# A two-layer attention and expert kernel: low halves by TensorE, zeros and bias moved, first steps reordered

## The reference, cut to what matters

```
x = x + L0_xattn(layernorm(x), ctx)   # cosine similarity of 64-wide projections: dots / (|v| |t|)
x = x + L0_ffn(layernorm(x))          # sigmoid gate, 8 experts in 4 groups, 2 groups then top 2 kept, shared expert
x = x + L1_xattn(layernorm(x), ctx)   # softmax cross attention, 16 heads of 8, biases on q, k, v, o
x = x + L1_ffn(x)                     # causal attention along the batch axis, then 8 GELU experts of 256, top 2
```

## Time and profile before

| | us |
|---|---|
| median of three runs | 919.15 (914.24 to 921.09) |
| the profiled execution's own time | 918.29 |
| its span, first to last instruction | 916.4 |
| busy: PE / DVE / ACT / POOL | 738.4 / 659.9 / 394.2 / 219.5 |
| mean granted TensorE clock, share of full | 0.928 |

### The profile page before, as it was taken

How to read it: one execution, slowest core, us unless ns; L and a number is a source line. 1 busy time by engine, 2 the same in 40 slices (tenths; PEclk the granted TensorE clock), 3 DMA queues, 4 the chain that set the end, 5 groups by cost and what they waited for, 6 DMA issues and landing times. The chain is left out here.

```text
span 916.4 us, 26258 instructions
## 1 busy us (share of the span) xinstructions
PE 738.4 (81%) x10100; PEld 550.8 (60%) x10100; DVE 659.9 (72%) x1808; ACT 394.2 (43%) x749; POOL 219.5 (24%) x338
## 2 busy tenths in 40 slices
PE   2568897887768787778888657787775999999997
PEld 1335555554456665666666425555553888888886
DVE  4479898887846888888888467887645656666653
ACT  2122222222313555555555435665542555545553
POOL 4333333335422023213100164334002001111100
PEclk9969999998787999999999859999996999999999
DMA  3000000320141211221120000000000000000000
GB/s 97 12 19 20 13 20 20 82 43 5 40 125 44 74 43 45 69 74 44 50 65 13 13 1 4 4 5 4 4 6 1 1 13 11 11 11 11 11 12 13
DMA packets 33082, 26.41 MB, mean 29 GB/s; under 512 B 9741, under 2 KB 29913, under 8 KB 32985
## 3 DMA queue, kind: packets, MB, share of 16 engines
q1 hardware_dynamic: 29944, 24.07, 9.9%
q10 hardware_dynamic: 3040, 0.98, 0.4%
HBM read 13.51 MB, written 7.34 MB: 23 GB/s over the span
## 5 line engine op out<-in xcount | busy, mean ns | idle before, releaser
L1826 PEld LDWEIGHTS bank<-w2r,hme 128*128 128x128 f32 x1024 | 132.3, 192 | 15.8 <-ACT hme L1679 1.4
L1826 PE MATMUL bank<-w2r,hme 128*128 128x128 f32 x1024 | 135.5, 276 | 0.0
L1679 ACT ACTIVATE hme<-bank,b 128x512 f32<-128x512 f32 x128 | 86.4, 687 | 96.3 <-PE bank L97 96.2
L960 ACT ACTIVATE P<-bank 128x512 f32<-128x512 f32 x128 | 76.7, 599 | 95.4 <-PE bank L1097 95.4
L1776 DVE SCALAR_TENSOR_TENSOR Xq<-bank,wgte,Xq 128x128 f32 (+1 forms) x256 | 72.0, 343 | 51.9 <-PE bank L1826 38.4
L1022 DVE TENSOR_SCALAR bank<-bank 128x512 f32<-128x512 f32 x128 | 89.0, 695 | 26.7 <-PE bank L1088 26.7
L1030 DVE TENSOR_REDUCE mx<-bank 128x4 f32<-128x512 f32 x128 | 87.1, 681 | 6.0 <-PE bank L1070 6.0
L1097 PE MATMUL bank<-mT,negsel 128*128 128x128 f16 x512 | 50.6, 222 | 44.6 <-DVE bank L1022 41.8
L502 ACT ACTIVATE w2r<-bank 128x512 f32<-128x512 f32 x40 | 23.9, 597 | 126.3 <-PE bank L803 92.2
L1097 PEld LDWEIGHTS bank<-mT,negsel 128*128 128x128 f16 x512 | 31.8, 98 | 55.7 <-issue 40.7
L814 PE MATMUL bank<-w_raw,hm 128*128 128x128 f32 x320 | 51.4, 313 | 8.6 <-DVE X L728 8.6
(11 more groups left out here) (375 smaller groups left out, 1796.3 us busy)
## 6 DMA issues: line engine op xcount, KB each, us to landing
cross_q<-qh SPq DMA_DIRECT2D x24, 128.0 KB
Q<-cross_q SPq DMA_DIRECT2D x8, 384.0 KB, 3.6
X<-in_x SPq DMA_DIRECT2D x8, 256.0 KB, 2.8
Xq<-X SPq DMA_DIRECT2D x32, 64.0 KB
cross_k<-kh SPq DMA_DIRECT2D x16, 128.0 KB
Yq<-Y SPq DMA_DIRECT2D x32, 64.0 KB
out_x<-Xq SPq DMA_DIRECT2D x32, 64.0 KB, 1.7
cload<-in_ctx SPq DMA_DIRECT2D x8, 192.0 KB, 2.6
```

The costliest lines, as they stand in the source:

```text
L960: act.activation(P[j][:], TB[j % 2][:], ACT.Exp, scale=SCALE).then_inc(s["p_ready"], 1)
L1679: act.activation(hm[:, p % HR], UP[p % RING][:], ACT.Gelu_apprx_tanh, bias=b1[:, p:p + 1]).then_inc(s["gelu"], 1)
L1826: last = pe.matmul(Y[e % 2][:, cols], hm[:, p % HR, cols], w2r[:, p], start=(p % 2 == 0 and i == 0), stop=(p % 2 == 1), skip_group_check=True)
```

## The change

Seven edits:

1. Layer 0, start: DVE's low halves of the expert and gate weights go from ahead of the first statistics to step -2, part 0 (`fill(0)`).
2. Layer 0: the zeros of K[0] and Q, six fills, go from POOL's `ahead` to DVE in step -2, part 1 (`fill(1)`).
3. Layer 0, step -1 alone: PE, ACT and DVE do `route(0, p)` ahead of `prep(1, p)`, and PE does `prep(1, 3)` (the broadcast of the norms) behind the routing's part 4.
4. The four copies of the last group to Xq go from the end of layer 0's SP list to the head of the cross attention's, ahead of the load of w2 and the gather.
5. Cross attention, chunks 2 to 7: the low halves of K and Q are made without DVE. PE leaves the bank's accumulation open, adds a product of the negated identity (`less`, a new fp16 tile that POOL writes) with the high half, ahead of the fourth score quarter, and ACT copies the bank to fp16 at the end of its step, behind the third exponential. New semaphores k_less and q_less.
6. The expert bias goes from step -1 to step 32, one before the last, into bank S0, with a wait for the last maxima; ACT's copies go to step 33.
7. POOL writes `less` between the V tiles and `ones16`.

```diff
@@ -148 +148 @@
     }
-    c["s"] = room.sems("""small_const w_hi w_lo zeros ones_v stats_a stats_b stats_c stats_d xn_ready xT_psum
+    c["s"] = room.sems("""small_const w_hi w_lo zeros ones_v k_less q_less stats_a stats_b stats_c stats_d xn_ready xT_psum
         xT_hi xT_lo k_psum k_hi k_lo k_out k_in q_psum q_hi q_lo q_out q_in v_psum v_ready s_psum s_max m_ready mT_psum mT_ready
@@ -183 +183 @@
-def cross_project(pe, c, cT, ident, ps, n, i):
+def cross_project(pe, c, cT, ident, ps, n, i, whole=True):
@@ -195 +195 @@
         pe.wait_ge(s["xT_lo"], n + 1)
-        split_product(pe, ps[:], [w[:] for w in c["wk"]], [tok(t, n) for t in cT]).then_inc(s["k_psum"], 1)
+        split_product(pe, ps[:], [w[:] for w in c["wk"]], [tok(t, n) for t in cT], stop=whole,
+                      skip_group_check=not whole).then_inc(s["k_psum"], 1)
     elif i == 2:
         pe.wait_ge(s["k_lo"], n + 1)
-        split_product(pe, ps[:], [w[:] for w in c["wq"]], [x[:] for x in c["xh"]]).then_inc(s["q_psum"], 1)
+        split_product(pe, ps[:], [w[:] for w in c["wq"]], [x[:] for x in c["xh"]], stop=whole,
+                      skip_group_check=not whole).then_inc(s["q_psum"], 1)
@@ -363 +365 @@
                 sp.dma_start(tile, source).then_inc(s["layer1_loaded"], 16)
-            for g in range(G):
+            for g in range(G - 1):
                 sp.wait_ge(s["x2_ready"], g + 1)
@@ -440 +442 @@
                 cross_normalise(pool, c, X, 0)
-                for t in c["K"][0] + c["Q"]:
-                    last = pool.memset(t[:].bitcast(mybir.dt.uint32), 0)
-                last.then_inc(cs["zeros"], 1)
                 cross_normalise(pool, c, X, 1)
@@ -500 +499 @@
                         act.activation(sg[:, p % 2, :], GP[p % 2][:], ACT.Silu).then_inc(s["sg_ready"], 1)
+                    if isinstance(g, int) and g == -1:
+                        route(g + 1, p)
                     if has(g + 2):
                         prep(g + 2, p)
-                    if has(g + 1):
+                    if has(g + 1) and not (isinstance(g, int) and g == -1):
                         route(g + 1, p)
@@ -543 +544 @@
             dve.tensor_tensor(wt0[1][:], P0[0:CT, DV:2 * DV], wt0[0][:], ALU.subtract).then_inc(s["w0t_split"], 1)
-            dve.wait_ge(s["w0_split"], 1)
-            dve.tensor_tensor(w0[1][:], w_raw[:, 0:2], w0[0][:], ALU.subtract)
-            dve.tensor_tensor(gw[1][:], gw_raw[:], gw[0][:], ALU.subtract).then_inc(s["w0_split"], 1)
...
             dve.wait_ge(s["consts"], 6)
@@ -558 +555 @@
                 last.then_inc(s["mv" + k], 1)
...
+            def fill(p):
...
+                if p == 0:
+                    dve.wait_ge(s["w0_split"], 1)
+                    dve.tensor_tensor(w0[1][:], w_raw[:, 0:2], w0[0][:], ALU.subtract)
+                    dve.tensor_tensor(gw[1][:], gw_raw[:], gw[0][:], ALU.subtract).then_inc(s["w0_split"], 1)
+                elif p == 1:
+                    for t in c["K"][0] + c["Q"]:
+                        last = dve.memset(t[:].bitcast(mybir.dt.uint32), 0)
+                    last.then_inc(cs["zeros"], 1)
@@ -663 +671 @@
                             dve.tensor_tensor(hm[:, p, :], sg[:, i, :], UP[:], ALU.mult).then_inc(s["hm_ready"], 1)
+                    if isinstance(g, int) and g == -2:
+                        fill(p)
+                    if isinstance(g, int) and g == -1:
+                        route(g + 1, p)
                     if has(g + 2):
@@ -823 +835 @@
                         up(g, p)
+                    if isinstance(g, int) and g == -1:
+                        route(g + 1, p)
+                        if p != 3:
+                            prep(g + 2, p)
+                        if p == 4:
+                            prep(g + 2, 3)
+                        continue
                     if has(g + 2):
@@ -875 +894 @@
         ones16 = sb("ones16", [128, 128], F16)
+        less = sb("less", [128, 128], F16)
+        kh, qh = c["kh"], c["qh"]
         c["K"][1] = [sb(f"K1_{j}", [128, 16 * S], F16) for j in range(U)]
@@ -912 +933 @@
+            for b in range(B - GB, B):
+                sp.dma_start(keep["Xq"][b::32], X[:, b, :]).then_inc(keep["xq_in"], 16)
             w2 = keep["w"]["w2"]
@@ -932 +955 @@
             last.then_inc(s["ones_v"], 1)
+            pool.tensor_scalar(less[:], ident[:], -1.0, None, ALU.mult)
             pool.memset(ones16[:], 1.0).then_inc(s["small_const"], 1)
@@ -986 +1010 @@
                     exp(b, 2)
+                low(n + 2, i)
...
+            def low(n, i):
...
+                if i == 1 and chunk(n):
+                    act.wait_ge(s["k_less"], n - 1)
+                    act.activation(kh[1][:], PB[:], ACT.Copy).then_inc(s["k_lo"], 1)
+                elif i == 2 and chunk(n):
+                    act.wait_ge(s["q_less"], n - 1)
+                    act.activation(qh[1][:], PB[:], ACT.Identity, bias=bq_raw[:]).then_inc(s["q_lo"], 1)
...
                 act.wait_ge(s["bias_psum"], 1)
-                act.activation(ex["b1"][:], F[:, 0:2 * NE], ACT.Copy)
-                act.activation(ex["rb"][:], F[:, 2 * NE:3 * NE], ACT.Copy).then_inc(s["bias_ready"], 1)
+                act.activation(ex["b1"][:], S0[:, 0:2 * NE], ACT.Copy)
+                act.activation(ex["rb"][:], S0[:, 2 * NE:3 * NE], ACT.Copy).then_inc(s["bias_ready"], 1)
...
             def prepare(n, i):
-                if n == 0 and i == 0:
+                if 4 * n + i == B + 1:
                     expert_bias()
@@ -1011 +1045 @@
             def prepare(n, i):
-                if i < 3 and chunk(n + 2):
+                if i == 0 and chunk(n + 2):
                     cross_low(dve, c, bq_raw, PB, n + 2, i)
@@ -1070 +1104 @@
                 last.then_inc(s["s_psum"], 1)
-                if b == 0:
-                    bias(j)
...
-            def bias(j):
...
-                for p in range(4 * j, 4 * j + 4):
-                    last = pe.matmul(F[:, p:p + 1], w1r[:, p], lnb2[:], start=True, stop=True)
-                if j == U - 1:
-                    last = pe.matmul(F[:, 2 * NE:3 * NE], lnbr[:], rT[:], start=True, stop=True)
-                    last.then_inc(s["bias_psum"], 1)
...
+            def bias():
...
+                for p in range(2 * NE):
+                    pe.matmul(S0[:, p:p + 1], w1r[:, p], lnb2[:], start=True, stop=True)
+                pe.matmul(S0[:, 2 * NE:3 * NE], lnbr[:], rT[:], start=True, stop=True).then_inc(s["bias_psum"], 1)
@@ -1111 +1141 @@
                 if i < 3 and chunk(n + 2):
-                    cross_project(pe, c, cT, ident, PB, n + 2, i)
+                    cross_project(pe, c, cT, ident, PB, n + 2, i, False)
                 elif i == 3 and chunk(n + 1):
...
                     last.then_inc(s["v_psum"], 1)
...
+            def subtract(n, i):
...
+                if i == 1 and chunk(n):
+                    pe.wait_ge(s["small_const"], 2)
+                    pe.wait_ge(s["k_hi"], n + 1)
+                    pe.matmul(PB[:], less[:], kh[0][:], start=False, stop=True, skip_group_check=True
+                              ).then_inc(s["k_less"], 1)
+                elif i == 2 and chunk(n):
+                    pe.wait_ge(s["q_hi"], n + 1)
+                    pe.matmul(PB[:], less[:], qh[0][:], start=False, stop=True, skip_group_check=True
+                              ).then_inc(s["q_less"], 1)
@@ -1141 +1183 @@
                     score_t(b, 1)
+                if b == B:
+                    pe.wait_ge(s["s_max"], U * B)
+                    bias()
                 if has(b - 2):
@@ -1158 +1203 @@
+                subtract(b // 4 + 2, b % 4)
                 if has(b1):
@@ -1167 +1213 @@
                     if b == 1:
-                        pe.wait_ge(s["bias_ready"], 1)
                         pe.wait_ge(s["small_const"], 2)
```

## The result

The changed kernel is faster by 2.9%. It takes 890.66 us (median of 4 runs, 889.09 to 892.03), beside 917.25 for the kernel before in the same measurement: ratio 0.9707, 95% interval 0.9661 to 0.9754. A second measurement on another occasion gives 891.67 and 0.9722 (0.9677 to 0.9767). Three executions far above all others of their kernel (996.84 us of the changed kernel in that second measurement, 948.08 of e_zeros, 1396.67 of the kernel before) are left out of every median and ratio of this document. The prediction was 898 with 889 to 907. The forecast gain was 21 us, the measured one 25 to 27.

What follows compares the result with a forecast made beforehand. The prediction took DVE to set the cross attention's step and a chain across PE, ACT, DVE and POOL to bound layer 0. Its terms summed to -21.0 us, from 918.3 to 897.3, given as 898 with range 889 to 907.

Steps and rivals of the forecast that it cites:

- Bound: Cross attention's steady stretch: DVE, in use 41.8 of 50 us, sets the step, and ACT has room.
- Start, -2.0: Layer 0's start: statistics ahead of the weight splits run at about 8.8 instead of 10.87, gaining 2.0 us.
- Step -1, +2.1: Layer 0, step -1: routing ahead of similarity makes the context ready 2.1 us later, a loss of 2.1 us.
- Rival (c): Layer 0: routing ahead costs step -1 nothing and step 0 starts 1 us sooner; whole 895 us, chance 0.13.
- The zeros, 0 and -4.0: Layer 0: fills cost nothing on DVE at the start; without POOL's fills step G-2 gains 4.0 us.
- rival (e): Layer 0's start: the moved fills make DVE hold the squares of group 0, +2.6; whole 901 us, chance 0.04.
- End of layer 0, -4.4: Boundary to the cross attention: SP's four copies move behind it, gaining 4.4 us.
- Start of the cross attention, -5.5: Without 34 bias passes between the first score quarters, the maxima's transpose comes sooner, gaining 5.5 us.
- Twelve steps, -10.9: Cross attention, steps 1 and 2 over six chunks: K's and Q's low halves off DVE gain 10.9 us.
- (a): Cross attention: steps don't shorten, because PE waiting for ACT replaces DVE; whole 909 us, chance 0.11.
- (d): Cross attention: PE's new wait for ACT drops its clock to 1.2 GHz; whole up to 942 us, chance 0.04.
- Bias at the end, +3.7: Cross attention's end: 34 bias passes take 4.05 us at full clock, net loss 3.7; at half clock 7.3.

Runs made afterwards that it cites:

- e_zeros: Changed kernel with the six zero fills back on POOL in step G-2 of layer 0: 896.25 us, ratio 0.9787.
- e_lows: Changed kernel with the low halves of K and Q in the cross attention back on DVE: 903.97 us, ratio 0.9860.
- e_low0: e_best with the third low half (transposed x, step 0 of each chunk) off DVE, result not the reference's: 869.82 us, ratio 0.9488.
- e_split: Changed kernel with DVE's subtractions for the low weight parts back ahead of the first statistics: 894.66 us, ratio 0.9755.
- e_prep: Changed kernel with step -1 of layer 0 back in its old order, similarity ahead of routing: 893.23 us, ratio 0.9753.
- e_copies: Changed kernel with the last group's four copies of X back ahead of the boundary to the cross attention: 897.59 us, ratio 0.9779.
- e_bstart: Changed kernel with the 34 bias passes back at the start of the cross attention: 893.96 us, ratio 0.9729.
- e_best: Changed kernel with step -1 in its old order and the bias spread over the cross attention's last eight steps: 886.45 us, ratio 0.9662.
- e_bias: Changed kernel with the 34 bias passes spread over the last eight steps of the cross attention: 890.00 us, ratio 0.9718.

## Why the prediction was right, step by step

- **Bound.** DVE sets the step of the cross attention, ACT and PE have room: shown by e_lows (12 us) and by e_low0.
- **Start, -2.0.** First statistics 1.7 to 2.1 us sooner, first addition 1.2 to 2.4 (e_split; and e_prep's 96.6 beside 98.19 and 99.01 of the kernel before). Right in mechanism, about right in size; the share of the clock in e_split's 1.2 is open.
- **Step -1, +2.1.** Right, and by the step that the forecast gave: the context is turned 2.2 us later, the first addition comes 2.7 later (e_prep). The two first terms nearly cancel, as the sum had it: 99.01 and 98.19 before, 99.15 and 99.53 after. Rival (c) is refuted at that place. Its mark in my own list was a clamp near 51.6; found were 51.17 and 51.61.
- **The zeros, 0 and -4.0.** Fills on DVE hidden (e_zeros, first addition unchanged); rival (e) didn't occur. The step with the stall is 4.05 shorter between the first profiles, 3.0 between the second, and 3.4 by e_zeros: right in mechanism, but the size is not fixed, since the stall is as long as what is left of the train (2.79 in the second profile of the kernel before). That is longer than the one instruction of the rule with which the forecast explained it; the last section comes back to this.
- **End of layer 0, -4.4.** 4.7 to 4.9, shown by e_copies.
- **Start of the cross attention, -5.5.** 6.3 to the transpose, 6.45 to the second clamp: the size was 0.8 to 0.95 too small, inside its bounds.
- **Twelve steps, -10.9.** 11.2 between the first profiles, 14.3 between the second ones. At the same amount of half clock it is 11.0 to 11.3, so the term was right; what the second pair has on top is the clock's. From the second chunk on steps 1 and 2 are at 6.52 to 6.58 and 6.53 to 6.54, except step 1 where the clock falls in step 0 (8.07 and 8.13 in the first profile, 8.12 in the second). The forecast read only a step 1 of 7.41; in the other places of that profile where the clock fell it took 7.90 to 8.47. Rivals (a) and (d) are refuted: the steps that the edit reaches are at 6.5, the clock is 0.98 and 0.99 there.
- **Bias at the end, +3.7.** The mis-sized term: 4.1 to 6.4. The passes themselves were sized rightly, 3.9 us wherever they ran at full clock. What failed is the step "here PE is at full clock" for the time behind it: the clock fell to 1.2 GHz while the passes ran or about 1 us behind them, and what follows ran at that level, which it did not in the kernel before (2 to 3 of its 13.4 to 13.7 us at half clock, 11.0 and 6.4 of the 19.8 and 17.8). My upper bound of 7.3 held.
- **What the sum had nowhere:** the stretch behind the cross attention, unchanged work, is 4.6 us shorter on the mean of two profiles each. Over 14 profiles it takes from 388.64 to 395.57. Both profiles of before are at the long end; of the other twelve only e_bstart, with 393.39, reaches them. That e_bstart shares with them the bias at the start is a hint and no more. The amount of half clock doesn't settle it: the stretch has 35 us of it in the second profile of the kernel before (393.18) and 35 in e_best (389.85). The last 190 us take the same time in all fourteen profiles, within 0.1 us; the differences arise ahead of them, nearly all in the causal attention. Which part belongs to the change stays open.

Against these terms stands the sum over the layer-0 edits: -3.9 forecast, and -1.3 on the mean of two profiles each, with 3.6 and 4.8 us between the two of one kernel (-2.3 if the mean of all seven profiles with this layer 0 is taken). The terms of the start and of the twelve steps of the cross attention are borne out by both pairs of profiles. That the sum of the whole came within 6 us is in part luck: the errors of single stages, in both directions, are of that size, and where the clock falls in one execution is not in the forecast.

What I can't explain: e_prep and e_bias show a stage gain of 2.7 and 4.3 to 6.4 us and no gain in time, both together 4 to 5.5 us by the ratios. e_prep's numbers fit the idea that a gain shifts where the clock falls in the stages behind it, but no run isolates that, and e_bias loses 1.4 to 2.6 us ahead of its edit, which this idea can't account for.

## What to carry to other kernels

Profile the same kernel twice before a difference of a few us in one stage is given a cause: here the same layer 0 took 257.0 and 261.8 us. Price a wait of PE by what it does to the clock behind it, not by its own length alone: cutting DVE's 0.7 us from step 0 saved 1.2 us there and up to 1.6 in a step that wasn't touched (e_low0, which is a schedule and not yet a kernel to use). A long train of small products can be spread over steps in which another engine sets the pace: the stage shows it (13.4 instead of 17.8 to 19.8 us at the end), the time of the whole doesn't, so count the gain there before you book it.

## What the runs showed of the hardware that I had not expected

- Two small DVE operations beside the same kind of POOL fills (128x1024 words, 0.95 us each) are held differently. The one on th (f32 in and out, 32 elements) waits for the whole rest of the train: 4.23, 4.24 and 2.79 us. The clamp of the maxima (f32 in, f16 out, 16 elements) waits for the one fill that runs: 0.71 and 0.73 us. The Trainium skill's page "SBUF — State Buffer", section "Who interferes with whom", has the exclusive lock for the length of one instruction. The clamp's numbers agree with it; th's, over three and more fills, are longer than it says. What makes the difference wasn't tried.
- PE's granted clock stays at full in all 31 steps of e_low0, with waits of up to 0.71 us in them, and is at half for a while behind some of the 2.45 us waits of the changed kernel's step 0 (those at 326.93 and 384.55, not those at 298.83 and 356.52). The same wait, in the same step of the same program, is followed by a fall or not (two of four here, one of four in the second profile, three of four in e_best).
